# A transformer block on one core: block 1's weights-times-values step moves from behind chunk 11 to behind chunk 9, the last score unit to chunk 9, and two steps of the values' way back to chunk 10

## The reference

```python
qkv = (x @ w_attn + b_attn)                      # 16 heads of 8 channels
scores = q k^T / sqrt(8) + slopes[h] * pos[s]    # ALiBi, causal mask
y = softmax(scores) @ v
attention = y @ w_proj + b_proj
...
e = argmax(softmax(x @ wr + br))                 # one of 8 experts for each token
experts = (gelu(x @ w1[e] + b1[e]) @ w2[e] + b2[e]) * top1 / (top1 + top2)
```

## Time and profile before

| | |
|---|---|
| time, median of three runs | 454.4 us (450.55, 454.4, 459.12) |
| the profiled execution's own time | 452.06 us |
| its span in the profile | 450.4 us |
| TensorE busy | 393.3 us (87%), mean granted clock 0.918 |
| VectorE, ScalarE, GpSimd busy | 302.1, 285.0, 241.9 us |

### The profile page before, as it was taken

One profiled execution on the slowest core, in us unless ns is written; L12 is line 12 of the kernel. 1 busy time (PEld: TensorE's weight loads), 2 busy tenths in 40 slices (PEclk: granted clock), 3 DMA queues, 4 the chain that ended last, 5 costly groups with the idle time before them and its releaser, 6 DMA issues.

```text
span 450.4 us, 11127 instructions
## 1 busy us (share of the span) xinstructions
PE 393.3 (87%) x3866; PEld 224.0 (50%) x3866; DVE 302.1 (67%) x495; ACT 285.0 (63%) x703; POOL 241.9 (54%) x369
## 2 busy tenths in 40 slices
PE   5856798889989993999999899989997997999974
PEld 3433333334434442999999744434443443444422
DVE  6796689986856784455555486877885884678501
ACT  4753346666846761866666777667775774667771
POOL 4441224478776884222222378795885984466321
PEclk8865859999987997999999999999999997899997
DMA  8897823385263225122222303272283163100000
GB/s 177 243 279 158 292 53 125 116 200 173 87 210 102 96 71 135 55 65 69 70 70 90 87 20 107 90 178 90 62 197 114 39 165 78 37 20 3 25 1 25
DMA packets 45980, 48.13 MB, mean 107 GB/s; under 512 B 6497, under 2 KB 40194, under 8 KB 45938
## 3 DMA queue, kind: packets, MB, share of 16 engines
q1 hardware_dynamic: 42064, 40.40, 33.2%
q0 software_dynamic: 3296, 6.76, 4.9%
q10 hardware_dynamic: 578, 0.40, 0.3%
HBM read 25.39 MB, written 21.89 MB: 105 GB/s over the span
## 4 chain that ended last, share of the span: by engine, by line
PE 60%; DMA 10%; DVE 10%; ACT 6%; POOL 5%; SPq 4%; issue 4%; ACTq 0%
PE ps L1193 14%; PE ps L1167 13%; PE ps L1125 8%; PE ps L1133 8%; DMA stack<-guard_p 6%; DVE mx L749 4%; PE ps L1051 4%; ACT probs L589 3%; PE ps L1016 2%; PE ps L1253 2%; POOL xs_sorted L948 2%; PE ps L1044 2%; SPq L380 2%; POOL probs L938 2%; SPq L390 1%
## 5 line engine op out<-in xcount | busy, mean ns | idle before, releaser
L589 ACT ACTIVATE probs<-ps 128x512 f32<-128x512 f32 (+2 forms) x384 | 190.9, 526 | 107.5 <-PE ps L1193 103.6
L749 DVE TENSOR_REDUCE mx<-ps 128x2 f32<-128x1024 f32 (+2 forms) x192 | 196.5, 1045 | 71.8 <-PE ps L1051 70.0
L1193 PE MATMUL ps<-stack 61*128 61x256 bf16 (+3 forms) x512 | 130.6, 314 | 21.5 <-ACT probs L589 10.6
L938 POOL TENSOR_SCALAR_AFFINE_SELECT probs<-probs 128x512 f32<-128x512 f32 x128 | 82.3, 647 | 95.1 <-ACT probs L589 93.3
L1044 PE MATMUL ps<-stack 59*128 59x256 bf16 (+3 forms) x512 | 103.4, 321 | 7.5 <-DMA stack<-qk_parts 3.8
L1167 PE MATMUL ps<-probs,vt 128*18 128x512 f32 (+3 forms) x1024 | 99.1, 461 | 3.2 <-POOL probs L938 3.2
L1193 PEld LDWEIGHTS ps<-stack 61*128 61x128 bf16 x512 | 38.4, 94 | 117.9 <-ACT probs L589 68.6
L1051 PE MATMUL ps<-tri,swap_b 64*128 64x64 bf16 (+1 forms) x384 | 72.8, 206 | 0.0
L1051 PE MATMUL ps<-tri,cbf 64*128 64x64 bf16 (+1 forms) x384 | 64.8, 205 | 0.0
L920 POOL DMA_DIRECT2D ys_sorted<-yst x39 | 21.1, 540 | 61.3 <-DVE yst L796 60.9
L566 ACT ACTIVATE hid<-ps,wcur 128x128 f32<-128x128 f32 x156 | 44.8, 375 | 0.5 <-PE ps L1125 0.5
(11 more groups left out here) (129 smaller groups left out, 387.2 us busy)
## 6 DMA issues: line engine op xcount, KB each, us to landing
stack<-qk_parts SPq DMA_DIRECT2D x64, 192.0 KB, 5.2
qk_parts<-qkp SPq DMA_DIRECT2D x16, 384.0 KB, 3.2
qk_parts<-qkp SPq DMA_DIRECT2D x16, 256.0 KB, 3.4
wall<-L_ffn_w SPq DMA_DIRECT2D x16, 256.0 KB
xs_sorted<-xst SPq DMA_DIRECT2D x1, 2496.0 KB, 12.1
xst<-xs_sorted SPq DMA_DIRECT2D x39, 64.0 KB, 1.8
ys_sorted<-yst POOLq DMA_DIRECT2D x39, 64.0 KB, 2.1
xt<-L_attn_x SPq DMA_DIRECT2D x8, 256.0 KB, 6.6
```

The source lines that it names most:

```text
L589: act.activation(p[:, e, slots[0]:slots[0] + ns], ps[:, ST_BANK[c % 2], 0:ns * w].rearrange("p (s w) -> p s w", s=ns), ACT.Exp).then_inc(e ...
L749: dve.tensor_reduce(mx[:, n % 2, :, slots[0]:slots[0] + k, tb], src, AX_X, ALU.max, negate=True).then_inc(mx_done, 1)
L938: pool.affine_select(out=p, in_=p, compare_op=ALU.is_ge, fill=0.0, base=0, pattern=[[0, G], [1, P]], channel_multiplier=-1).then_inc(p_mas ...
L1193: last = pe.matmul(ps[:, ST_BANK[c % 2], i * w:(i + 1) * w], stack[at:at + N_STACK, b % 2, 1, 2 * g + s, P * sb_:P * (sb_ + 1)], stack[at: ...
```

## The change

Only the order of TensorE's instructions in a group changes, and two conditions in VectorE's program. Score unit 5 goes from chunk 10 to chunk 9; w1 goes from behind chunk 11 to behind chunk 9 (and behind score unit 5); `y_back` and the second half of the projection go from behind chunk 9 to behind chunk 10. VectorE's `normal` and the projection's addition are moved from c = 10 to c = 11, where nothing stands between: VectorE's own row of instructions is the same as before, as are those of ScalarE, GpSimd and SP.

```diff
-                if (g, c) == (0, 10) and b:
+                if (g, c) == (0, 11) and b:
                     normal(2 * b - 1)
...
-                if (g, c) == (2, 10) and n < GROUPS:
+                if (g, c) == (2, 11) and n < GROUPS:
                     normal(2 * b)
...
-                elif c % 2 == 0 and n + LEAD < GROUPS:
-                    score_unit(n + LEAD, c // 2)
+                elif (c in (0, 2, 4, 6, 8, 9)) and n + LEAD < GROUPS:
+                    score_unit(n + LEAD, (c + 1) // 2)
...
-                if c == 11 and n < GROUPS:
+                if c == 9 and n < GROUPS:
                     weigh(n, 1)
...
-                if (g, c) == (0, 9) and b:
+                if (g, c) == (0, 10) and b:
...
-                if g == 1 and c in (8, 9) and b:
+                if g == 1 and c in (8, 10) and b:
...
-                if (g, c) == (2, 9) and n < GROUPS:
+                if (g, c) == (2, 10) and n < GROUPS:
```

More of the change, by code:

```diff
@@ L842, in dve_at @@
                     split_qk(b + 2, g // 2)
-                if (g, c) == (0, 10) and b:
+                if (g, c) == (0, 11) and b:
                     normal(2 * b - 1)
-                if (g, c) == (1, 10) and b:
+                if (g, c) == (1, 11) and b:
                     dve.wait_ge(proj_ps, b)
@@ L1248, in pe_at @@
                     last.then_inc(y2_ps, 1)
-                if g == 1 and c in (8, 9) and b:
+                if g == 1 and c in (8, 10) and b:
                     if c == 8:
                         pe.wait_ge(y2_copied, b)
-                    for t in range(2 * (c - 8), 2 * (c - 8) + 2):
+                    for t in range(c - 8, c - 8 + 2):
                         last = pe.matmul(ps[:, MISC, t * C:(t + 1) * C], yn2[:, t * P:(t + 1) * P], wpj[:],
                                          start=True, stop=True)
-                    if c == 9:
+                    if c == 10:
                         last.then_inc(proj_ps, 1)
-                if (g, c) == (2, 9) and n < GROUPS:
+                if (g, c) == (2, 10) and n < GROUPS:
                     if b + 2 < NB:
```

## The result

The changed kernel takes 470.75 us, the median of four runs (468.03 to 475.41), against 452.75 us for the kernel before in the same comparison. The ratio is 1.039, with a 95% interval from 1.030 to 1.049: slower by 18 us. The profiled execution took 468.03 us, its span is 466.4 us. The forecast was 461.0 with a range to 468.0, so the result lies outside it, on the side that it leaned to.

The account below looks back on a forecast made before the run. TensorE, busy 87% of the span, was taken to bound the kernel. The groups' terms summed to +8.2 us, 460.3 us on the profiled execution and 462.6 on the median; the forecast was 461.0, range 453 to 468.

Parts of the forecast that it names:

- Groups with transposes: End of groups g = 0 and 2: chunk 1 waits for exp 11, cost 0.55 us, as worked for group 18.
- g = 1: End of groups g = 1: chunk 1 at 4.20 instead of 3.77 us behind chunk 8, cost 0.43 us.
- g = 3: End of groups g = 3: w1 fills the wait for exp 8, chunk 1 at 2.75 instead of 2.90, gain 0.15 us.
- Late masks: Groups with n % 3 = 1, bias addition ahead of m1: w1 waits for m1, cost 1.26 us in group 22.
- 7 and 10: Groups with GpSimd behind with scatters: its next mask of block 3 waits for exp 11, cost 0.35 and 0.65 us.
- Hidden ends: Ends of groups 3, 4, 15, 16, 19, 20, 23, 24: guard DMA waits up to 2.3 us swallow them, cost zero.
- Rival A, the clock: Added waits of about half a microsecond make TensorE's clock fall once or twice more: 464 us, with two 468; chance 0.20.
- B: Exps of chunks 10 and 11 are short, TensorE's later work takes up the slack: 452 to 454 us; chance 0.14.
- C: Early w1 fills waits at chunks 10 and 11 in all groups, faster: 447 us; chance 0.08.

Follow-up runs that it names:

- back_behind_11: The changed kernel with the four transposes and the projection's second half behind chunk 11 instead of chunk 10: 464.7 us.
- bias_later: The changed kernel with GpSimd's bias addition moved from c = 6 to c = 10: 471.9 us, ratio 1.053.
- change_guard_first: The changed kernel with the second half of the queries' and keys' loads issued behind the guard's load: 463.6 us, ratio to before 1.028.
- change_both: The changed kernel with those loads behind the guard's load and GpSimd's bias addition at c = 10: 454.1 us, ratio 1.007.
- guard_first_split: The kernel before with loads behind the guard's load, bias addition at c = 8, w1 in two halves in g = 3 groups: 437.0 us, ratio 0.963.

## Why the prediction was wrong

**Groups with transposes: right.** For group 18 the forecast had w1 at 1.12, chunk 10 at 1.89, chunk 11 at 2.68 and chunk 1 at 3.46; the profile has 1.13, 1.90, 2.70 and 3.46. The mechanism was named and sized, and back_behind_11 confirms it by taking it away. One sign of it was foreseen wrongly: TensorE's waits for exps were to rise by some 6 us and rose by 0.6, because the loss at chunk 1 is recorded as busy time of the score unit.

**g = 1: right where the mask is early.** 0.43 was forecast, 0.46 measured in group 21. In groups 5 and 9 it was 0.82, in group 13 0.69, for the reason that follows. In group 29 it was 0.76: no score unit follows there, so that before chunk 1 had come together with chunk 0, and all of its new wait counts.

**g = 3: wrong in sign, small.** A gain of 0.15 was forecast; group 27 lost 0.07 (chunk 0 at 2.57, chunk 1 at 2.97). The exp of chunk 10 was released 0.1 later than I took, and exp 11 follows exp 10 on ScalarE. Groups 15 and 23 lost 0.25 to 0.29; of this 0.19 lies between chunk 1 and chunk 8, and its cause stays open.

**Late masks: this is the step that failed.** The forecast let each mask m1 end where it ended in the trace of before, and charged w1's wait for it only in group 22 (1.26) and, loosely, in 7 and 10 (1.0). But it had said itself that GpSimd's mask of block 3 waits for exp 11, which the change makes later: in group 18 that mask starts 3.47 behind chunk 8, where it started at 2.50. GpSimd works in order: in group 22 the guard's parts, two gathers, two steps on their results, the mask of block 0 and the bias addition stand between that mask and the next m1, 7.5 us in either kernel. So m1 moved later against TensorE by 0.4 us, and by more in groups 5 and 9, in the groups where GpSimd has no slack, and w1 now stands right behind it. Measured with the clock full: 1.68 in group 22, 1.02 in group 26 (0.55 forecast), 1.37 in group 19 (a hidden end), 0.82 in groups 5 and 9. In group 10 m1 is not later (it ends 1.82 behind chunk 8, before 1.81); there the forecast charged 0.65 for a w1 that waits until 1.88, and 1.29 was measured. In total TensorE waits 7.9 us longer for masks. bias_later takes 5.9 us of these waits away, nearly all in groups with n % 3 = 1, which shows what they wait for; that m1 itself became later is shown by the equal distances.

Averaged over the two profiles of either kernel, the groups between 5 and 29 that had full clock in both lose 10.7 us together, where the forecast had 7.4 for them. Of the 3.3 us between, 2.6 lie in groups 5, 9, 10, 13, 22 and 26, where w1 waits for its mask, and 0.3 in group 29. Groups 7 and 25 could be compared only in part; with about 1.4 and 0.5 for these, an estimate, it is near 13, against 8.2 forecast.

**Hidden ends: right.** The forecast set groups 3, 4, 15, 16, 19, 20, 23 and 24 to zero. Averaged in the same way, groups 19 and 20 together lost 0.25 (1.37 lost, 1.12 regained), 15 and 16 gained 0.2, 23 and 24 lost 0.04, 3 and 4 gained 0.4. So the term was right to within 0.4 us a pair, and change_guard_first shows that there was something to hide (3.6 us in groups 13 to 23).

**Rival A, the clock: in part.** Some 5 of the 18 us are not in those groups. About 3 lie in the sample: in the later comparisons the kernel before has medians of 454.5 to 456.2 us, over 50 runs 455.5 (one run of 575.6 us at a mean clock of 0.554 left out), and the changed kernel has 470.6 over its eight, which is 15 us. In the first pair of profiles 3.2 us lie ahead of group 0, where nothing was changed. In the fourteen profiles group 0 starts between 38.5 and 42.7 us, on average at 41.3 in the eight with all of w1 behind chunk 9 and at 39.5 in the other six, so that whether this is chance alone stays open.

What is left fits the clock, which the forecast had put at nothing. Its mean is 0.918 over the 50 runs of the kernel before and 0.907 over the eight of the changed one; one minus the clock, times the span, gives 37 and 44 us, so by this estimate it cost at most some 7 us. In the two profiles of each kernel it was even (76.0 and 93.5 us at half clock against 86.8 and 83.1), and the spans still differ by 10.9 us on average: the waits are the larger part. The stretches change place from run to run in one and the same kernel, but one goes with the change. In group 7, w1 waits 2.37 to 2.59 us for its mask in the five profiles that have it early and the bias addition at c = 6, and in all five a stretch of 10.2 or 13.7 us at half clock begins within 1.2 us of the end of that wait. In the other nine profiles the longest wait for a mask there is 1.15 to 1.58 us, and a stretch of 6.8 or 10.2 us followed in four. That speaks for a link between the late mask and the clock; it is too few to prove it.

The rule that the forecast drew on from the Trainium skill, "TensorE: Matmul & The Clock Gate", section "A second HAM failure mode: psum-queue depth-cycling", that short idles in a kernel that cycles through PSUM banks make the clock go up and down, isn't borne out for waits of about half a microsecond: groups 13 to 23 of change_both have seven waits from 0.15 to 0.62 us, and a clock of 1.00 throughout.

**Rivals B and C** are out: no group at full clock and outside the guard waits got faster by more than 0.1 us, and the measured 470.75 us are far from B's 452 to 454 us and from C's 447.

## What to carry to other kernels

Before moving a step forward, ask what it covered where it stood, and what will cover that now: here 0.77 us of weighing hid two short exps of 0.38 us. Then follow the delayed result through the in-order row of every engine that waits for it, round to the next iteration, until it meets the moved step again; a forecast that shifts only the engine whose code was edited is too small. And a large wait that hides losses is worth removing first: taking the guard's small load out from behind four of eight large ones brought the kernel before to a ratio of 0.979, and showed what the change really cost.

## What was not expected of the hardware

Two of four products take as long as all four. w1 is four products of 18 columns, on four strips of 32 columns of the array; it took 0.77 us from its start to the next chunk. Two of them alone, in guard_first_split, took 0.76 us (316.99 to chunk 10 at 317.75), and the other two again 0.76 (318.20 to 318.96). So the four strips work beside each other here, and splitting such a step by heads doubles it. In the g = 3 groups the second 0.76 us took back what the filled wait had given: 8.44 us with the split, 8.43 without.

A DMA of 4 KB that is issued behind eight of 192 KB took 4.90 us to land, and 6.19 and 6.27 us in two other groups; with four of the eight behind it, two waits of at most 1.0 us were left of six, both ahead of the first two groups, and neither of these loads had been moved.
